# State space outputs, second normalisation, dispatch, expert tiles and last sum in one stage

## The chip, the cores and the metric

The kernel runs on one core of a Trainium2 chip. The metric is the device time of one execution in microseconds (us). PE is TensorE, DVE VectorE, ACT ScalarE, POOL GpSimd, SP SyncE, the engine that issues most of the plain DMAs.

## The reference

Sixteen sequences of 256 tokens with 128 features pass through four layers. Each adds to x the normalised output of its sublayer: `x = x + layernorm(f(layernorm(x)))`. The sublayers are a differential attention, two blocks of window attention with feed forward, a state space model, and a mixture of experts. The change lies in the last two:

```python
# state space: u = x W_in' + b_in; h_t = h_(t-1) A + u_t Bm'
return jnp.einsum('bsn,hn->bsh', hs, C) + D

# mixture of experts, 8 experts, 2 for each token
logits = xt @ router_w.T
topk_vals, topk_idx = jax.lax.top_k(logits, 2)
g = sigmoid(topk_vals);  g = g / (g.sum(-1, keepdims=True) + 1e-10)
for e in range(8):
    ge = jnp.sum(jnp.where(topk_idx == e, g, 0), axis=-1)
    h = silu(xt @ w_gate[e]) * (xt @ w_up[e])
    out = out + ge[:, None] * (h @ w_down[e])
```

## The kernel before

X and F are two arrays in SBUF that hold all tokens: 32 tiles of 128 tokens. A group is four tiles, so there are eight groups. Everything is float32. The program is a row of blocks. In a block each engine has its own list of instructions, worked off in order, with semaphores between engines; a block ends when all its engines are done, and only then does the next one begin. POOL waits at the end of its lists for the DMAs it has issued.

The four blocks at the end are these.

**State space** (`state_space`, L1351). PE turns and projects F, then eight levels of a doubling scan run over the states `Hs`. The last loop makes the outputs: for each of 16 sequences PE makes two products of the states with C into a PSUM buffer (L1467), and DVE adds D and writes F (L1422). The buffers are two, so PE and DVE alternate.

**Second normalisation and dispatch** (`dispatch`, L1511). Per group g: `inner.statistics` of F on DVE (L627 to L634), `power` on POOL for 1/sqrt (L620), `shifts` on DVE (L639), `apply` on ACT (L647), the addition to X on DVE (L1634), the same normalisation of X (`outer`) into `pay`, then `turn` on PE (L1664), ACT's move of it to SBUF (L1655), `route` on PE (L1672), `choose` on DVE (L1580 to L1607: the two best experts, one-hot rows, running counts), `ranks` on PE (L1683 to L1687) and `place` on DVE (L1612 to L1622: the row number of each token in its expert's region). Last, `send` on POOL scatters the four tiles to DRAM, `mx_rows`, once for each choice: eight indirect DMAs for a group (L1558), 64 in all. DVE goes through its parts in a loop in which each part lags the one before by a step. POOL's loop is `inner.power(g)`, `outer.power(g - 2)`, `send(g - 5)`. PE's is `turn(g)`, `route(g - 1)`, `ranks(g - 2)`. POOL ends by waiting for all sends.

**Expert tiles** (`mixture_of_experts`, L1714). DVE first makes a table of which expert and which rows belong to each of 72 slots of 128 rows (`tiles_of_experts`, L1786 to L1811, which raises `listed`), then the gates (L1816 to L1826). SP waits for `listed`, loads row numbers to registers, and loads tiles (`mx_xin`, L1764). Per slot: PE turns the tile (L1919), one product gives gate and up (L1926), ACT makes silu (L1881), DVE multiplies (L1848), PE turns (L1934), ACT moves, PE makes the down product (L1942), DVE copies it to `y` (L1855), and POOL scatters it to `mx_results` (L1773), four buffers of `y` being in turn. POOL ends by waiting for all scatters.

**Last sum.** SP loads both results of each token (L1980, L1981), ACT and DVE weigh and add them (L2003, L2016), the sum is normalised, POOL adds it to X (L1994), SP stores (L1984).

## Time and profile before

| | us |
|---|---|
| median of 3 runs | 2083.77 |
| lowest and highest | 2082.64, 2086.82 |
| the profiled execution | 2089.91 |
| its span, first to last instruction | 2088.1 |
| busy: PE, DVE, ACT, POOL | 1708.9, 1544.3, 1361.4, 876.0 |

The page cuts the span into 40 equal slices of 52.2 us; a digit is the busy share in tenths:

```profile
PE   4999999999999936999996977999996939242990
DVE  2888989889898856999995566999995573632444
ACT  2888888888888844888884325888884252411554
POOL 3555655556555543333231232323331240473554
PEclk9999999999999966999998988999998978555995
```

PEclk is the TensorE clock granted, in tenths of 2.4 GHz, so a 5 is 1.2 GHz. The last seven or eight slices are the blocks told of above. In an answer of the trace an instruction stands with its start, its duration, its engine and line, output and inputs, and in brackets the idle time of its engine just before it and what ended that.

### The profile page before, as it was taken

Reading aid. Unit: us, or ns where it says so; the run is one execution under the profiler, and the core shown is the slowest. Engines: PE = TensorE matmul, PEld = TensorE weight load, DVE = VectorE, ACT = ScalarE, POOL = GpSimd, SP = SyncE. Lnnn points to the kernel's source line nnn. Section 1 sums busy time; section 2 is a strip of 40 time slices with the busy share of each in tenths; the row PEclk is TensorE's granted clock in tenths of the full one; section 3 lists DMA queues with packets and bytes.
Section 4 is the critical chain, followed back from the end, with each engine's and each line's share of the span. In section 5 each row is a group of like instructions: output and inputs, shape, how many; then the busy total and the mean of one; then the engine's idle time right before and its main releaser. Section 6 shows DMA issues by size and latency. Waiting matters only on the chain. (4 is left out here: it accounts for less than half of the span.)

```text
span 2088.1 us, 39231 instructions
## 1 busy us (share of the span) xinstructions
PE 1708.9 (82%) x12344; PEld 1128.4 (54%) x12410; DVE 1544.3 (74%) x4156; ACT 1361.4 (65%) x4708; POOL 876.0 (42%) x816
## 2 busy tenths in 40 slices
PE   4999999999999936999996977999996939242990
PEld 2555555555555514777774545777774515241660
DVE  2888989889898856999995566999995573632444
ACT  2888888888888844888884325888884252411554
POOL 3555655556555543333231232323331240473554
PEclk9999999999999966999998988999998978555995
DMA  6990000000000000000000100000001100012324
GB/s 203 185 180 6 2 2 1 2 2 1 2 2 2 2 0 6 16 16 11 17 16 20 30 12 6 12 16 16 17 11 25 30 2 1 15 47 53 83 64 129
DMA packets 102525, 65.90 MB, mean 32 GB/s; under 512 B 27698, under 2 KB 93874, under 8 KB 102322
## 3 DMA queue, kind: packets, MB, share of 16 engines
q1 hardware_dynamic: 97970, 54.40, 13.1%
q0 software_dynamic: 4352, 8.99, 1.3%
q8 instruction: 103, 1.69, 0.4%
q14 instruction: 100, 0.82, 0.1%
HBM read 19.50 MB, written 30.24 MB: 24 GB/s over the span
## 5 line engine op out<-in xcount | busy, mean ns | idle before, releaser
L411 ACT ACTIVATE a_E<-a_psS,a_nm 128x128 f32<-128x128 f32 (+1 forms) x1028 | 418.8, 428 | 31.3 <-DVE a_nm L245 28.9
L216 POOL TENSOR_SCALAR a_aT<-a_dT 128x384 f32<-128x384 f32 x256 | 309.4, 1208 | 299.1 <-PE a_psO L529 187.5
L245 DVE TENSOR_REDUCE a_nm<-a_psS 128x2 f32<-128x256 f32 (+1 forms) x514 | 260.2, 547 | 43.7 <-PE a_psS L496 43.0
L492 PE MATMUL a_psS<-a_kT,a_qm 32*128 32x128 f32 (+1 forms) x2064 | 240.6, 351 | 5.6 <-issue 3.7
L270 DVE SCALAR_TENSOR_TENSOR a_d<-a_E,a_cf 128x128 f32<-128x128 f32 (+1 forms) x512 | 219.3, 468 | 27.9 <-DVE a_cf L259 1.4
L411 ACT ACTIVATION_READ_ACCUMULATOR a_E<-a_psS,a_nm 128x1 f32 x1028 | 219.9, 214 | 0.0
L830 POOL TENSOR_TENSOR b0rn<-b0ss,minus_half 128x16 f32<-128x16 f32 x36 | 107.1, 2976 | 224.1 <-DVE b0ss L866 224.1
L830 POOL TENSOR_TENSOR b1rn<-b1ss,minus_half 128x16 f32<-128x16 f32 x36 | 107.1, 2976 | 223.3 <-DVE b1ss L866 223.3
L420 ACT ACTIVATE a_dT<-a_psT 128x384 f32<-128x384 f32 x256 | 126.7, 495 | 74.4 <-PE a_psT L505 71.4
L492 PEld LDWEIGHTS a_psS<-a_kT,a_qm 32*128 32x128 f32 x2064 | 136.6, 186 | 55.8 <-issue 35.6
L505 PE MATMUL a_psT<-ident,a_d 128*128 128x128 f32 x768 | 132.4, 281 | 6.2 <-DVE a_d L270 0.3
L505 PEld LDWEIGHTS a_psT<-ident,a_d 128*128 128x128 f32 x768 | 87.7, 141 | 34.7 <-DVE a_d L270 28.4
L496 PE MATMUL a_psS<-causal,identb 128*128 128x256 bf16 x516 | 101.8, 279 | 0.0
L1773 POOL DMA_INDIRECT mx_results<-mx_y,mx_targetu x72 | 68.6, 953 | 72.3 <-DVE mx_y L1855 63.5
L964 ACT ACTIVATE b0E<-b0psS,b0nm 128x128 f32<-128x128 f32 x260 | 91.8, 376 | 10.0 <-DVE b0nm L894 10.0
L964 ACT ACTIVATE b1E<-b1psS,b1nm 128x128 f32<-128x128 f32 x260 | 91.8, 376 | 8.7 <-DVE b1nm L894 8.7
L1077 PE MATMUL b0psQ<-wqk,b0hT 128*128 128x512 f32 x148 | 81.3, 676 | 16.9 <-DVE b0part L875 12.0
L1077 PE MATMUL b1psQ<-wqk,b1hT 128*128 128x512 f32 x148 | 80.5, 670 | 16.7 <-DVE b1part L875 11.3
L1848 DVE TENSOR_TENSOR mx_h<-mx_psG,mx_sl 128x256 f32<-128x256 f32 x72 | 30.6, 425 | 72.3 <-issue 37.8
L1046 PEld LDWEIGHTS b0psS<-b0kT,b0qm 128*128 128x128 f32 x528 | 72.1, 198 | 18.2 <-issue 16.3
L1046 PEld LDWEIGHTS b1psS<-b1kT,b1qm 128*128 128x128 f32 x528 | 71.8, 197 | 18.2 <-issue 16.3
L518 PE MATMUL a_psO<-a_dT,a_vp 128*32 128x256 f32 x516 | 81.2, 393 | 0.6 <-ACT a_dT L420 0.6
(353 smaller groups left out, 4392.5 us busy)
## 6 DMA issues: line engine op xcount, KB each, us to landing
mx_rows<-mx_blank SPq DMA_DIRECT2D x9, 2080.0 KB, 32.3
mx_xin<-mx_rows SPq DMA_DIRECT2D x72, 65.0 KB
b0v<-b0v SPq DMA_DIRECT2D x34, 128.0 KB, 2.3
b1v<-b1v SPq DMA_DIRECT2D x34, 128.0 KB
F<-mx_results SPq DMA_DIRECT2D x8, 256.0 KB, 4.8
mx_second<-mx_results SPq DMA_DIRECT2D x8, 256.0 KB, 5.3
out_dram<-X SPq DMA_DIRECT2D x8, 256.0 KB, 2.3
f0z<-F SPq DMA_DIRECT2D x9, 128.0 KB
```

The costliest lines, as they stand in the source:

```text
L216: pool.tensor_scalar(aT[:, s, :], dT[:, s, :], 0.0, None, ALU.max).then_inc(positived.sem, 1)
L245: ins = dve.tensor_reduce(nm[:, s, t, :], psS[:, s, :, (0, P)[t]:(P, 384)[t]], axis=AX.X, op=ALU.max, negate=True)
L270: ins = dve.scalar_tensor_tensor(out=d[:, s, c0:c1], in0=E[:, s, 1, c0:c1], scalar=cf[:, s, t:t + 1], in1=E[:, s, 0, c0:c1], op0=ALU.mult, ...
L411: ins = act.activation(E[:, s, m, c0:c1], psS[:, s, m, c0:c1], ACT.Exp, bias=nm[:, s, t, m:m + 1], accum_out=Z[:, p, h, t, m:m + 1])
L420: act.activation(dT[:, s, :], psT[:, s, 0:384], ACT.Copy).then_inc(evaced.sem, 1)
L492: pe.matmul(psS[:, s, m, c0:c1], qm[rows, p, a, r, t * P:(t + 1) * P], kT[rows, p, a, 0:c1 - c0], start=(t == 0), stop=False)
L496: ins = pe.matmul(diagonal, identb[:, :], causal[:, :].unsqueeze(1).broadcast_to([P, 2, P]), start=False, stop=True)
L505: ins = pe.transpose(psT[:, s, c * P:(c + 1) * P], d[:, s, c * P:(c + 1) * P], ident[:, :])
L830: pool.tensor_tensor(rn[:, t, :], ss[:, t, :], minus_half[:, 0:2 * H], ALU.pow).then_inc(rn_ready.sem, 1)
L964: ins = act.activation(E[:, s, n, :], psS[:, s, n * P:(n + 1) * P], ACT.Exp, bias=nm[:, s, n:n + 1], accum_out=Z[:, s, n:n + 1])
L1046: ins = pe.matmul(psS[:, s, n * P:(n + 1) * P], qm[:, p, g, n].rearrange("p j q -> p (j q)"), kT[:, p, g, KEYS[n]:KEYS[n] + P], start=Fals ...
L1077: ins = pe.matmul(psQ[:, n * W:(n + 1) * W], hT[:, p, t * P:(t + 1) * P], wqk[:, n * W:(n + 1) * W], start=True, stop=True)
```

## The change

Everything from the state space's outputs on becomes one block. `dispatch` is gone; `state_space` ends with the scan and leaves its states in `states`. `mixture_of_experts` does the rest: 

- The outputs are made two sequences at a time, which is one group: `outputs(b)` on PE and `outputs(g)` on DVE, which goes on to the group's statistics.
- The order of the first three groups (LEAD) is written out on DVE, ACT, PE and POOL. Behind that DVE's loop is: outer shifts of g + 2, inner shifts of g + 3, choose(g + 1), outputs(g + 4), place(g + 1), residual(g + 3). PE's is: outputs, route(g + 1), turn(g + 2), ranks(g + 1). POOL's is: send(g), inner power of g + 4, outer power of g + 3.
- Behind the loops the table of slots, the gates and the slots follow on each engine in its own list. SP waits for `listed`, loads registers, then waits for all sends (`sent`) ahead of its first load; it waits for all scatters ahead of loading results. POOL waits for neither.
- Means and variances (`mv`) have a buffer for each group. PSUM is shared: the router's buffers are those of the expert tiles, and those of the outputs serve as `psT` and `psC`.

```diff
-        self.mv = ctx.enter_context(nc.sbuf_tensor(name + "mv", [P, 2, G, 2], FP32))
+        self.mv = ctx.enter_context(nc.sbuf_tensor(name + "mv", [P, self.groups, G, 2], FP32))
...
-            for b in range(BATCH):
-                dve.wait_ge(y_full, b + 1)
-                dve.tensor_tensor(f_of(b), psX[:, b % 2, 0:T].rearrange("p (t n) -> p t n", t=QT),
-                                  dv[:, :].unsqueeze(1).broadcast_to([P, QT, D]), ALU.add).then_inc(y_ready, 1)
...
+        psX = psG = ps("psG", [P, 2, 512])
+        psR = psH = ps("psH", [P, 2, 512])
+        psK = psY = ps("psY", [P, 2, 512])
+        psO = ps("psO", [P, 2, 512])
+        psT, psC = psO[:, 0, :], psO[:, 1, :]
...
+        @block.sync
+        def _(sp):
+            sp.wait_ge(listed, 1)
+            for i in range(SLOTS):
+                if i % SHARE == 0:
+...
+                if i == 0:
+                    sp.wait_ge(sent, 16 * 2 * TILES)
...
+            for k in range(4):
+                sp.wait_ge(scattered[k], 16 * (SLOTS // 4))
+            o = out.rearrange("b (t p) d -> p (b t) d", p=P)
+            for g in range(GROUPS):
+                sp.dma_start(ln.tiles(F, g), result(0, g)).then_inc(fetched[g], 16)
...
         @block.gpsimd
-            for g in range(GROUPS + 5):
+            for g in range(LEAD):
+                inner.power(pool, g)
+            outer.power(pool, 0)
+            outer.power(pool, 1)
+            inner.power(pool, LEAD)
+            outer.power(pool, 2)
+            pool.wait_ge(filled, 16 * fills)
+            for g in range(GROUPS):
+                send(g)
+                if g + 4 < GROUPS:
+                    inner.power(pool, g + 4)
+                if g + 3 < GROUPS:
+                    outer.power(pool, g + 3)
...
-            pool.wait_ge(sent, 16 * 2 * TILES)
...
         @block.vector
+            def outputs(g):
+                for b in (2 * g, 2 * g + 1):
+                    dve.wait_ge(o_full, b + 1)
+                    dve.tensor_tensor(F[:, QT + b * QT:QT + (b + 1) * QT, :],
+                                      psO[:, b % 2, 0:T].rearrange("p (t n) -> p t n", t=QT),
+                                      dv[:, :].unsqueeze(1).broadcast_to([P, QT, D]), ALU.add).then_inc(o_used, 1)
+                dve.wait_ge(o_used, 2 * g + 2)
+                inner.statistics(dve, g)
...
+            outputs(0)
+            outputs(1)
+            inner.shifts(dve, 0)
+            outputs(2)
+            inner.shifts(dve, 1)
+            residual(0)
+            inner.shifts(dve, 2)
+            residual(1)
+            outer.shifts(dve, 0)
+            outputs(3)
+            outer.shifts(dve, 1)
+            residual(2)
+            choose(0)
+            place(0)
+            for g in range(GROUPS):
+                if g + 2 < GROUPS:
+                    outer.shifts(dve, g + 2)
+                if g + 3 < GROUPS:
+                    inner.shifts(dve, g + 3)
+                if g + 1 < GROUPS:
+                    choose(g + 1)
+                if g + 4 < GROUPS:
+                    outputs(g + 4)
+                if g + 1 < GROUPS:
+                    place(g + 1)
+                if g + 3 < GROUPS:
+                    residual(g + 3)
+            tiles_of_experts()
+            gates()
...
         @block.scalar
+            for g in range(LEAD):
+                inner_apply(g)
+            outer_apply(0)
+            move_turned(0)
+            outer_apply(1)
+            for g in range(GROUPS):
+                if g + 1 < GROUPS:
+                    move_turned(g + 1)
+                if g + 2 < GROUPS:
+                    outer_apply(g + 2)
+                if g + 3 < GROUPS:
+                    inner_apply(g + 3)
...
         @block.tensor
+            for b in range(2 * LEAD + 2):
+                outputs(b)
+            turn(0)
+            route(0)
+            turn(1)
+            ranks(0)
             for g in range(GROUPS):
+                if g + 4 < GROUPS:
+                    outputs(2 * g + 8)
+                    outputs(2 * g + 9)
+                if g + 1 < GROUPS:
+                    route(g + 1)
+                if g + 2 < GROUPS:
+                    turn(g + 2)
+                if g + 1 < GROUPS:
+                    ranks(g + 1)
+            pe.wait_ge(seen_ready, GROUPS + 1)
+            pe.matmul(psC[:, 0:NE], c["ones"][:, :], seen[:, GROUPS, :], start=True, stop=True).then_inc(counted, 1)
+            pe.wait_ge(listed, 1)
...
```

## Rows read from the trace of the kernel before

**Rows 1.** Windows by stage: stretch, length, busy PE PEld DVE ACT POOL, clock, DMA, GB/s.

```profile
1775.40:1809.05 33.65, 8.53 (x38) 7.90 (x38) 23.24 (x157) 13.92 (x34) 11.33 (x10) 0.50 0.00 1
1809.05:1902.40 93.35, 30.16 (x138) 29.36 (x138) 30.95 (x215) 16.17 (x38) 68.60 (x70) 0.50 0.14 45
1902.40:1909.46 7.06, 0.00 (x0) 0.00 (x0) 0.00 (x0) 0.00 (x0) 0.00 (x0) 0.50 0.03 9
1909.46:1916.38 6.92, 0.57 (x2) 0.50 (x2) 5.86 (x16) 1.54 (x2) 0.00 (x0) 0.50 0.00 1
1916.38:2043.34 126.96, 121.24 (x648) 81.09 (x648) 50.43 (x174) 62.67 (x181) 68.60 (x72) 0.97 0.28 76
2043.34:2051.05 7.71, 0.00 (x0) 0.00 (x0) 0.00 (x0) 0.00 (x0) 0.00 (x0) 0.57 0.02 9
2051.05:2088.10 37.05, 0.00 (x0) 0.00 (x0) 23.30 (x112) 22.73 (x64) 18.91 (x16) 0.50 0.64 171
```

**Rows 2.** Timeline of DVE, first outputs and statistics: start, duration, instruction, idle before.

```profile
1762.28 0.87 DVE L1422 TENSOR_TENSOR F<-s_psX,s_wD 128x256 f32<-128x256 f32 x2 [0.80 <-PE s_psX L1467]
...
1775.39 0.20 DVE L1625 COPY mx_pay<-mx_token 128x32 f32<-128x32 f32 x1 [0.64 <-PEq L1362]
...
1775.48 0.87 DVE L627 BATCH_NORM_STATS2 n2ist<-F 128x6 f32<-128x128 f32 x4
...
1776.88 0.86 DVE L627 BATCH_NORM_STATS2 n2ist<-F 128x6 f32<-128x128 f32 x4
```

**Rows 3.** Timeline, one group's way from residual over router to placing.

```profile
1780.14 0.69 DVE L1634 TENSOR_TENSOR X<-X,F 128x512 f32<-128x512 f32 x1 [0.25 <-ACT F L647]
...
1794.06 0.19 DVE L1580 COPY d_lo<-d_psR 128x32 f32<-128x32 f32 x1 [4.40 <-PE d_psR L1672]
...
1796.53 0.86 DVE L627 BATCH_NORM_STATS2 n2ist<-F 128x6 f32<-128x128 f32 x4
...
1804.40 0.55 PEld L1683 LDWEIGHTS d_psK<-d_both,mx_tri 128*128 128x128 f32 x2
...
1806.18 0.61 PE L1687 MATMUL d_psK<-mx_seen,mx_ones 128*128 128x32 f32 x2
...
1807.13 0.18 DVE L1612 TENSOR_TENSOR d_rank<-d_psK,mx_region 128x32 f32<-128x32 f32 x1
...
1860.85 0.60 ACT L1655 ACTIVATE d_xT<-d_psX 128x512 f32<-128x512 f32 x1 [0.72 <-PE d_psX L1664]
```

**Rows 4.** Timeline, POOL's sends: first, ninth, 49th, last.

```profile
1809.05 1.24 POOL L1558 DMA_INDIRECT mx_rows<-mx_pay,d_posu  x1 [7.76 <-issue]
...
1821.38 1.57 POOL L1558 DMA_INDIRECT mx_rows<-mx_pay,d_posu  x1 [0.18 <-issue]
...
1882.49 0.96 POOL L1558 DMA_INDIRECT mx_rows<-mx_pay,d_posu  x1 [3.78 <-DVE d_posu L1622]
...
1901.44 0.95 POOL L1558 DMA_INDIRECT mx_rows<-mx_pay,d_posu  x1 [0.30 <-issue]
```

**Rows 5.** Groups by line and form, 1775 to 1909 us: all 64 sends.

```profile
L1558 POOL DMA_INDIRECT mx_rows<-mx_pay,d_posu x64 | 62.4, 975 | 32.4 <-issue 26.0 <-DVE d_posu L1622 6.4
```

**Rows 6.** Waits of DVE, 1809 to 1903 us: total, times, longest.

```profile
DVE d_rank L1612 <- remote: 8.2, 2, 5.5
```

**Rows 7.** Timeline, SP's first load of token tiles.

```profile
1916.38 8.65 SPq L1764 DMA_DIRECT2D mx_xin<-mx_rows  x15
```

**Rows 8.** Window behind the last send, columns as in rows 1.

```profile
1903.50:1904.00 0.50, 0.00 (x0) 0.00 (x0) 0.00 (x0) 0.00 (x0) 0.00 (x0) 0.50 0.00 0
```

**Rows 9.** Timeline, one scatter (POOL) and the copy four slots later (DVE).

```profile
2027.00 0.95 POOL L1773 DMA_INDIRECT mx_results<-mx_y,mx_targetu  x1 [0.79 <-DVE mx_y L1855]
...
2032.98 0.28 DVE L1855 COPY mx_y<-mx_psY 128x128 f32<-128x128 f32 x1
```

**Rows 10.** Timeline, a gate and up product on PE, early and late in the expert tiles.

```profile
1922.50 1.91 PE L1926 MATMUL mx_psG<-m_experts,mx_xT 128*128 x2
...
2024.62 1.02 PE L1926 MATMUL mx_psG<-m_experts,mx_xT 128*128 x2
```

More of the change, by code:

```diff
@@ L1359, in state_space @@
     ident = consts["ident"]
[L1360 removed]
+    win, bin_, bm, am, amT = (w[k] for k in ("W_in", "b_in", "Bm", "A", "AT"))
     with ExitStack() as ctx:
@@ L1575, in _, with residual @@
             own_steps = Steps(dve, own)
+            def outputs(g):
[6 more added lines that the diff above has]
+                inner.statistics(dve, g)
+            def residual(g):
+                dve.wait_ge(applied, g + 1)
+                xs = inner.tiles(X, g)
+                dve.tensor_tensor(xs, xs, inner.tiles(F, g), ALU.add).then_inc(added, 1)
+                dve.wait_ge(added, g + 1)
+                outer.statistics(dve, g)
             def choose(g):
@@ new lines, in aim @@
+            def aim(n):
+                mark, last = own_steps.mark, own_steps.last
+                share = slice(n * SHARE, (n + 1) * SHARE)
+                ring = slice(n * SHARE % RING, n * SHARE % RING + SHARE)
+                for i in range(n * SHARE, (n + 1) * SHARE):
+                    x_of(dve, i)
+                mark(dve.tensor_tensor(other[:, share], xin[:, ring, D + 1], expert[:, share], ALU.not_equal))
+                last()
+                mark(dve.scalar_tensor_tensor(out=target[:, share], in0=other[:, share], scalar=float(TILES * P),
+                                              in1=xin[:, ring, D], op0=ALU.mult, op1=ALU.add))
+                last()
+                dve.tensor_tensor(targetu[:, share], target[:, share], c["trash"][:, share], ALU.min)\
+                   .then_inc(aimed, 1)
@@ new lines, in _ @@
+            tiles_of_experts()
+            gates()
+            gate_up(0)
+            for i in range(SLOTS + 1):
+                if i % SHARE == 0 and i < SLOTS:
+                    aim(i // SHARE)
+                if i + 1 < SLOTS:
+                    gate_up(i + 1)
+                if i >= 1:
+                    move_y(i - 1)
+            for g in range(GROUPS + 1):
+                if g < GROUPS:
+                    dve.wait_ge(weighted, g + 1)
+                    for t in range(NT):
+                        z = ln.tiles(F, g)[:, t, :]
+                        ins = dve.scalar_tensor_tensor(out=z, in0=second[:, g * NT + t, :],
+                                                       scalar=sg[:, g * NT + t, 1:2], in1=z, op0=ALU.mult, op1=ALU.add)
+                    ins.then_inc(summed, 1)
+                    dve.wait_ge(summed, g + 1)
+                    ln.statistics(dve, g)
+                if g >= 1:
+                    ln.shifts(dve, g - 1)
@@ L1644, in _, with inner_apply @@
         @block.scalar
         def _(act):
[L1646 to L1655 removed]
+            def inner_apply(g):
+                inner.apply(act, g, inner.tiles(F, g)).then_inc(applied, 1)
@@ new lines, in _ @@
+            outer_apply(0)
+            move_turned(0)
+            outer_apply(1)
+            for g in range(GROUPS):
+                if g + 1 < GROUPS:
[4 more added lines that the diff above has]
+                    inner_apply(g + 3)
+            act.wait_ge(hot_ready, GROUPS)
+            act.activation(sg[:, :, :], top[:, :, 0:2], ACT.Exp, scale=-1.0).then_inc(expd, 1)
+            move_x(0)
@@ new lines, in _ @@
+            silu(0)
+            for i in range(SLOTS):
+                if i % 2 == 0 and i + 2 < SLOTS:
+                    move_x(i // 2 + 1)
+                if i + 1 < SLOTS:
+                    silu(i + 1)
+                move_h(i)
+            act.wait_ge(gated, 1)
+            for g in range(GROUPS + 2):
+                if g < GROUPS:
+                    act.wait_ge(fetched[g], 32)
+                    for t in range(NT):
+                        ins = act.activation(ln.tiles(F, g)[:, t, :], ln.tiles(F, g)[:, t, :], ACT.Copy,
+                                             scale=sg[:, g * NT + t, 0:1])
+                    ins.then_inc(weighted, 1)
+                if g >= 2:
+                    ln.apply(act, g - 2, second[:, of(g - 2), :]).then_inc(normal, 1)
@@ L1657, in _, with outputs @@
         @block.tensor
         def _(pe):
+            def outputs(b):
+                n, j = divmod(b, SEQ)
+                group = slice(NS * n, NS * n + NS)
+                if b >= 2:
+                    pe.wait_ge(o_used, b - 1)
+                for t in range(QT):
+                    ins = pe.matmul(psO[:, b % 2, t * P:(t + 1) * P], states[group, j, t * P:(t + 1) * P], cT[group, :],
+                                    start=True, stop=True)
+                ins.then_inc(o_full, 1)
             def turn(g):
```

583 lines of the change are left out of this document (219 added, 364 removed).

## The prediction

> **What bounds the kernel now.** I read the page first: its slices show that PE is near 90% until about 1690 us, and that behind this every engine has holes. The change touches only that last part, so the windows by stage come next [rows 1]. They show four things. The second normalisation with the dispatch lasts from 1775.40 to 1902.40 us, and its larger part, 93.35 us, is the time from POOL's first send to its last. Behind it lie 7.06 us in which nothing computes, then 6.92 us in which only the table of expert tiles is made, then 126.96 us of expert tiles with PE busy for 121.24. Then come 7.71 us of nothing, and 37.05 us of the last sum. Ahead of all this stand the 16 output products of the state space, which the timeline shows as a stage of their own, 1762.28 to the next block's first instruction at 1775.39 [rows 2].
>
> The second look is at what POOL, which sets the end of the dispatch, waits for. One send occupies 1.263 us: from the 49th to the 64th there are 15 intervals in 18.95 us [rows 4], with DVE idle. Eight make a group, 10.1 us. From the first to the ninth send there are 12.33 us, so the two rs powers in between cost 2.2 us, 1.1 each [rows 4]. POOL idled for DVE's places only 6.4 us in all [rows 5]. So 64 sends plus powers are the floor there, and what can be gained is an earlier first send and whatever stands between the last send and the first load.
>
> **The first send.** Before, it starts at 1809.05 [rows 4]. For the changed kernel I lay DVE's written order out with measured pieces. The recurrence's last addition ended 0.80 before the first output addition, at 1761.48, and a block change costs 0.64 [rows 2]; DVE's first output addition then starts 0.80 later, at 1762.9. One call of outputs(g) is two additions (0.87 together), a gap of 0.04, and one statistic, 1.40 from start to start [rows 2]: 2.3 us. One residual(g) is an addition of 0.69 plus the same 1.40 with its gap: 2.1 us [rows 2, 3]. A shift is below 0.1. Three outputs, two residuals and three shifts put outer.shifts(0) at 1774.3. From an outer shift to the router's result DVE waited 4.40 us (ACT's apply, PE's turn and route) [rows 3]; in the new order ACT's move to SBUF stands in this chain too, with its wait of 0.72 and its 0.60 [rows 3], so choose(0) starts at 1774.3 + 4.4 + 1.3 = 1780.0. By then DVE has done outputs(3) and residual(2) (to 1778.9), so they are free. Choosing takes 2.47 us (1794.06 to 1796.53), the hot rows being ready 2.1 in; the ranks take 2.4 on PE (1804.40 to 1806.79) [rows 3]; from the first instruction of place to the first send it is 1.9 us (1807.13 to 1809.05) [rows 3, 4]. That gives 1780.0 + 2.1 + 2.4 + 0.1 + 1.9 = 1786.5. **Part one: 22.5 us earlier.** Some 13 of these are the outputs stage, which no longer stands alone: PE's eight first products run ahead under DVE's statistics, and the other eight under the sends.
>
> **The sends.** Three more powers fall between first and last send (nine in place of six), as the first send is earlier: +3.3. The 6.4 us of idle go if DVE stays ahead. While powers are coupled (they stand behind send(g) in POOL's queue, and DVE's next shifts wait for them), DVE's turn is shifts 0.16, choose 2.47, outputs 2.3, place 0.8, residual 2.1, and a wait of about 0.6 for the ranks, which stand behind turn(g+2) on PE (the turn ends 3.1 into the DVE's turn, the ranks 2.4 later, and place could start at 4.9): 8.5 us, against the 10.1 of POOL's eight sends. The cover is thus 1.6 us a group, and where it is gone, each us of DVE costs one. PE has the two products and the route ahead of turn and ranks, and both waits are long fulfilled. The last three groups have no powers behind the sends: place(7) comes near 1859, eight us before its send is due. The span becomes 93.35 - 6.4 + 3.3 = 90.3, ending at 1876.8. **Part two: 3.1 us.**
>
> **From the last send to the first load.** Before, these are 13.98 us (1902.40 to 1916.38) [rows 1, 7]. The table (6.92 us) now runs on DVE behind place(7), near 1860 to 1868, under the last sends; if that cover is gone it costs up to 6.9. Exp's table load and the gates lie there too, and SP's register loads stand ahead of its wait for the sends. What is left is the landing of the last send. The trace shows no wait for a send alone, so I bound it. From below: bytes stop 1.1 us behind the issue's end [rows 8], and some half us for the semaphore makes 1.6. From above: the scatter issued until 2027.95 must have landed before the copy at 2032.98, which did not wait for it: 5.0 [rows 9]. I take the middle, 3.3, since the empty 7.06 are nearer to the upper end and hold a block change as well; with 0.3 for SP, 3.6. **Part three: 13.98 - 3.6 = 10.4 us** (8.7 to 12.1).
>
> The Trainium skill, DMA: Bandwidth & Descriptors, section on the anatomy of one DMA on the gpsimd path, gives about 2.0 us of fixed cost to a DMA, mostly the write receipt. Counted from the issue's start that would be some 1.2 us behind its end, an estimate from that page, and the whole would come out about 4 us lower than my sum; the empty 7.06 us do not contradict it, but do not show it.
>
> **The expert tiles.** Same instructions, same PSUM banks in another naming, POOL's scatters unchanged: 126.96 us [rows 1]. PE has a pause ahead of them as before, so its cold start should be the same. **Zero.**
>
> **Results to last sum.** POOL's wait and the block change go; SP waits itself for the same last scatter. Before 7.71 us [rows 1], now 3.6 by the same landing: **4.1 us** (2.4 to 5.8). The last sum keeps its 37.05; eight slots in place of two for mean and variance change no duration.
>
> **How the numbers follow.** 22.5 + 3.1 + 10.4 + 4.1 = 40.1 us. Against the profiled execution: 2088.1 - 40.1 = 2048.0 of span. The profiled execution took 2089.91 with what lies around the span, 6.1 above the median of the three runs, 2083.77. The differences are of stages that don't depend on that, so the forecast is 2083.77 - 40.1 = 2043.7 us. Chance 0.68.
>
> **Rivals.**
> First, DVE late for POOL. In the late dispatch DVE waited 8.2 us in two waits for something the profile calls remote, once 5.5 [rows 6], though PE had finished; this is where most of POOL's 6.4 came from. With a cover of 1.6 a group such pauses could fall into the coupled part. All of the idle back gives 2043.7 + 6.4 = 2050; the full 8.2 twice over, less cover, about 2056. For it: the sends now begin 22 us sooner, under more DVE work. Against: in the last three groups the cover is 8 us. Chance 0.18.
> Second, POOL slowed by DVE beside it: each send longer than 1.263. If an output addition (0.43) held a send for its whole length, the eight under the sends cost 3.5, with the statistics of four groups (1.4 each) 9: 2053. Against: the first eight sends, beside DVE's statistics, kept the pace of the late ones beside an idle DVE (12.33 less two powers is the same 10.1) [rows 4]. Chance 0.07. The Trainium skill names such a mechanism, in SBUF — State Buffer, section on the two separate sides: GpSimd and a DVE instruction in a two-port mode lock each other out of a shared port, and descriptors written on GpSimd starve. By that rule the change would be hurt; the trace speaks against it here.
> Third, the barrier's removal doing nothing: the table comes late behind a stalled DVE and the landing is at its upper end. 6.9 + 3.4 back: 2054. Chance 0.03.
> Fourth, slower: PE stays at its low clock in the expert tiles. Early in the stage a gate and up product took 1.91, late 1.02 [rows 10]. The stage is PE's, 121.24 us in 72 slots or 1.7 each [rows 1], so a slot at the low clock of 1.2 GHz adds some 1.5. From 27 slots on the gain is gone; all 72 would give about 2150. Before, the stage's mean grant was 0.97 [rows 1], so the rise came early, and nothing in PE's work there changes. Chance 0.03.
> No measurable change (0.2% is 4.2 us, about what a measurement of this kernel can tell): 0.01.
>
> Chances: faster 0.96, same 0.01, slower 0.03. The range takes the landing's bounds on both sides (3.4 each way), two us for the layout of the first groups, two for the median, and the first two rivals above: 2036.5 to 2056.
>
> **What would show it.** The first send near 25 us behind the recurrence's last addition, where it was 47.6; 64 sends within 90 us without a wait for a place; the first load 2 to 5 us behind the last send; the first fetch of results the same behind the last scatter; the tile stage at 127 us. A coupled turn above 12.4 us would refute the cover; a first load later than 5.3 us behind the last send, the landing; a tile stage over 130 us, the zero there.

## The result, and the profile after

The changed kernel takes 2049.78 us, the median of 4 runs (2048.32 to 2053.39); the kernel before takes 2083.97 us beside it (4 runs, 2082.64 to 2086.82). The ratio is 0.9837, 95% interval 0.9819 to 0.9854: 1.6% faster, 34 us. Forecast were 2043.7 us, in a range of 2036.5 to 2056. Run again on another chip (below), it gave 0.9841 (0.9826 to 0.9856).

The profiled execution took 2051.13 us, its span is 2049.3. It is shown by the same stretches as [rows 1]: from the recurrence's last addition to the first send, the sends, to SP's first load of tiles, to the end of the last scatter, to SP's first fetch, to the end of POOL's last addition, to the end. The columns are stretch, length, busy time of PE, PEld, DVE, ACT and POOL, PE's granted clock, DMA share, GB/s.

```profile
1761.87:1786.36 24.49, 14.64 (x67) 12.61 (x67) 18.39 (x108) 10.21 (x25) 8.39 (x8) 0.56 0.00 1
1786.36:1878.92 92.56, 39.74 (x177) 37.81 (x176) 48.70 (x296) 21.34 (x50) 71.71 (x73) 0.50 0.14 46
1878.92:1880.60 1.68, 0.00 (x0) 0.00 (x0) 0.00 (x0) 0.00 (x0) 0.00 (x1) 0.50 0.12 40
1880.60:2007.96 127.36, 121.00 (x648) 80.60 (x648) 49.81 (x171) 62.77 (x181) 69.07 (x72) 0.97 0.28 76
2007.96:2009.31 1.35, 0.00 (x0) 0.00 (x0) 0.00 (x0) 0.00 (x0) 0.00 (x0) 0.50 0.14 49
2009.31:2043.13 33.82, 0.00 (x0) 0.00 (x0) 23.29 (x112) 22.74 (x64) 18.93 (x16) 0.50 0.66 176
2043.13:2049.34 6.21, 0.00 (x0) 0.00 (x0) 0.00 (x0) 0.00 (x0) 0.00 (x1) 0.50 0.20 58
```

Beside before and the forecast, in us:

| stretch | before | forecast | after | after less before |
|---|---|---|---|---|
| recurrence's last addition to first send | 47.57 | 25.0 | 24.49 | -23.1 |
| first send to end of last | 93.35 | 90.3 | 92.56 | -0.8 |
| to the first load | 13.98 | 3.6 | 1.68 | -12.3 |
| expert tiles | 126.96 | 126.96 | 127.36 | +0.4 |
| last scatter to first fetch | 7.71 | 3.6 | 1.35 | -6.4 |
| last sum, to the end | 37.05 | 37.05 | 40.03 | +3.0 |

With 0.4 us by which the recurrence ended later, these make the 38.8 us between the two spans. The medians lie only 34.2 apart: the profiled execution of before was 6 us above its median, that of after 1.4. Three lines want an explanation: the sends hardly gained, the last sum lost 3 us that no step of mine held, and the two gaps closed further than any landing time I had assumed.

The way to the first send, on the timeline (start, duration, engine, instruction, idle time before it in brackets):

```profile
1763.20 0.87 DVE L1662 TENSOR_TENSOR F<-mx_psO,s_wD 128x256 f32<-128x256 f32 x2 [0.48 <-PE mx_psO L1927]
...
1774.32 0.15 DVE L639 SCALAR_TENSOR_TENSOR n2oshift<-n2omv,n2ors 128x4 f32<-128x4 f32 x1
...
1779.92 0.19 DVE L1678 COPY mx_lo<-mx_psH 128x32 f32<-128x32 f32 x1 [1.07 <-PE mx_psH L1944]
```

The first outer shift stands at 1774.32 (forecast 1774.3), choose(0) at 1779.92 (forecast 1780.0), the first send at 1786.36 (forecast 1786.5). As the recurrence ended 0.39 us later than in the trace of before (1761.87 for 1761.48), each station came 0.4 to 0.5 us sooner behind it than forecast. In all these 24.49 us DVE waits four times, the longest times 2.0 us for the first ranks and 1.1 us for the router.

Among the sends, one wait was in no forecast. The last ranks and the last group's first send:

```profile
1859.18 0.61 PE L1959 MATMUL mx_psY<-mx_seen,mx_ones 128*128 128x32 f32 x2
...
1867.27 0.19 DVE L1710 TENSOR_TENSOR mx_rank<-mx_psY,mx_region 128x32 f32<-128x32 f32 x1 [9.43 <-remote]
1869.02 0.96 POOL L1621 DMA_INDIRECT mx_rows<-mx_pay,mx_posu  x1 [2.45 <-DVE mx_posu L1720]
```

PE's matmul is listed as over at 1859.79, but DVE starts at 1867.27, and POOL idles 2.45 us for it. In [rows 6] DVE's d_rank waited in the same manner, 5.5 us once, and the 6.4 us of POOL's idle time in [rows 5] came from that.

The block ends, last. By line and engine's sequencer, with min/median/max ns, the drain with which POOL leaves a block: the dispatch (L1519), the tiles (L1714) and the last sum (L1709) of before, then the only one of after.

```profile
L1519 POOLq DRAIN  x1: 5298/5298/5298, 1903.9 to 1903.9; - x1
```
```profile
L1714 POOLq DRAIN  x1: 5927/5927/5927, 2044.9 to 2044.9; - x1
```
```profile
L1709 POOLq DRAIN  x1: 1374/1374/1374, 2084.1 to 2084.1; - x1
```
```profile
L1507 POOLq DRAIN  x1: 7278/7278/7278, 2041.8 to 2041.8; - x1
L1507 SPq COMPARE_BRANCH  x1: 38/38/38, 2045.5 to 2045.5; - x1
```

A drain's record begins while POOL's last instruction still runs. In before's last block POOL's addition ran through 1.29 of the 1.37 us, so the drain itself is 0.1, and the end of that kernel came 2.70 us behind POOL's last addition:

```profile
2085.40:2088.10 2.70, 0.00 (x0) 0.00 (x0) 0.00 (x0) 0.00 (x0) 0.01 (x1) 0.50 0.47 134
```

In after the addition ended at 2043.13 and the drain at 2049.12, 5.98 us later, at the very end: SP's last wait, for the output's landing, was over at 2045.5, and the kernel ended at 2049.3. The two blocks of before that hold sends or scatters had 5.30 and 5.93 us. So the suspicion before the experiments: **not the barrier and not the landing, but POOL's drain is what a block end costs here, and the change removed two and moved one to the end.**

### The profile page after: what moved, and what is told of

Read it like the earlier page. It is cut to its first block and busy times, and to the rows that moved or that the text cites. A ratio compares the mean times of both kernels' runs of the same rounds, so it can differ in the third digit from the quotient of the medians.

```text
span 2049.3 us, 39274 instructions
## 1 busy us (share of the span) xinstructions
PE 1719.8 (84%) x12410; PEld 1128.4 (55%) x12410; DVE 1544.9 (75%) x4156; ACT 1363.4 (67%) x4708; POOL 877.9 (43%) x816
## 5 line engine op out<-in xcount | busy, mean ns | idle before, releaser
L1046 PEld LDWEIGHTS b0psS<-b0kT,b0qm 128*128 128x128 f32 x528 | 71.9, 198 | 18.2 <-issue 16.3
L1046 PEld LDWEIGHTS b1psS<-b1kT,b1qm 128*128 128x128 f32 x528 | 71.9, 197 | 18.2 <-issue 16.3
```

What stands on the lines that cost most here:

```text
L1046: ins = pe.matmul(psS[:, s, n * P:(n + 1) * P], qm[:, p, g, n].rearrange("p j q -> p (j q)"), kT[:, p, g, KEYS[n]:KEYS[n] + P], start=Fals ...
```

## Experiments

Each is compared with the kernel before by runs on the same chip; chips differ by some us, so ratios are compared, and stretches of the traces.

**1. The last sum in a block of its own.** The changed kernel, one block end put back:

```
-            for k in range(4):
-                sp.wait_ge(scattered[k], 16 * (SLOTS // 4))
...
+            for k in range(4):
+                pool.wait_ge(scattered[k], 16 * (SLOTS // 4))
...
+        first_blocks.close()
+        block = ctx.enter_context(nc.Block())
```

> The changed kernel, with only the last sum put back into a block of its own (POOL waits for the scatters before the block ends, as before the change). Theory A: a block in which POOL issued software DMAs ends with a POOL drain of 5.3 us (seen in the trace of before: POOL's wait for the sends was over at 1903.75, its drain stood until 1909.22), whatever is still in flight. Then the gap from the last scatter's end to the first fetch goes from 1.36 us to about 7.7, and the tail from POOL's last addition to the end goes from 6.17 us to about 2.7, because the last block holds no software DMA: net +2.9 us, about 2052.7. Rival B, the gap before was mostly the landing of the scatter, and the long tail of the changed kernel has another cause (the out transfer): the gap grows by a block change of 0.7 us, the tail stays at 6.2: +0.7 us, about 2050.5. Rival C, the barrier costs 6.35 us and the tail is the out transfer's: gap 7.7, tail 6.2, about 2056.

Measured: 2052.42 us, ratio 0.9854 (0.9835 to 0.9873). The gap, the last sum and the tail, and the two drains:

```profile
2004.77:2012.51 7.74, 0.00 (x0) 0.00 (x0) 0.00 (x0) 0.00 (x0) 0.00 (x0) 0.60 0.02 8
2012.51:2046.95 34.44, 0.00 (x0) 0.00 (x0) 23.39 (x112) 22.73 (x64) 18.87 (x16) 0.50 0.63 173
2046.95:2049.67 2.72, 0.00 (x0) 0.00 (x0) 0.00 (x0) 0.00 (x0) 0.00 (x1) 0.50 0.47 131
```
```profile
L2007 POOLq DRAIN  x1: 5952/5952/5952, 2006.3 to 2006.3; - x1
...
L1507 POOLq DRAIN  x1: 1362/1362/1362, 2045.7 to 2045.7; - x1
```

Both sides of theory A: the gap is 7.74 and the tail 2.72. The drain has moved from the end to the block end, it hasn't vanished. B and C fall, since each kept the tail at 6.2. The loss in time against the changed kernel, 0.0017 in the ratio, lies within the two intervals; the trace's stretches carry the verdict.

**2. Both block ends put back**, so that only the merged outputs and the order are left of the change (POOL waits for the sends at the end of the dispatch's block, as before).

> The changed kernel with both block ends put back, so that only the merge of the state space outputs with the dispatch and the written-out order stay. Theory A: first send about 24.5 us behind the recurrence's last addition and the sends 92.6 us long, as in the changed kernel; from the last send's end to the first load 13.5 to 14.5 us in place of 1.68 (landing 1.35, drain 5.3, table of tiles 6.5, block change), then the gap of the last scatter 7.7 and the tail 2.7: about 12.3 + 2.9 = 15.2 us above the changed kernel, 2065. Rival: the barriers were hidden behind the landing of the transfers (gap 4 to 5 us more at each): 2057 or less. Rival: part of the early first send is lost when the blocks are apart: above 2070.

Measured: 2060.44 us, ratio 0.9893 (0.9876 to 0.9909).

```profile
1763.54:1788.02 24.48, 14.63 (x66) 12.60 (x67) 18.39 (x108) 10.20 (x25) 8.39 (x8) 0.56 0.01 1
1788.02:1878.27 90.25, 39.38 (x175) 37.41 (x174) 41.76 (x278) 19.80 (x48) 71.52 (x73) 0.50 0.14 47
1878.27:1892.26 13.99, 0.57 (x2) 0.50 (x2) 5.87 (x16) 1.54 (x2) 0.00 (x0) 0.50 0.02 5
...
2018.74:2026.45 7.71, 0.00 (x0) 0.00 (x0) 0.00 (x0) 0.00 (x0) 0.00 (x0) 0.53 0.02 9
```

Every stretch came as theory A has it: 24.5, 14.0, 7.7, a tail of 2.7. Against the changed kernel the two gaps and the tail make 15.2 us; from the recurrence to the end the trace is 13.6 us longer than that of experiment 5, as its tiles and its last sum were somewhat shorter. The medians make 13 (2060.44 to 2047.39, with before at 2080.47 and 2081.28 beside them), the two ratios (0.9893 and 0.9841) 11. The 2065 of the expectation counted from the first chip's times, on which everything is some 3 us longer. The two merges of blocks are thus worth some 11 to 14 us and the first part of the change some 20 to 22. The sends took 90.25 us here, the 90.3 of the prediction.

**3. Who waits for the landing.** The kernel before, with POOL's two waits moved to SP in the next block:

```
-            pool.wait_ge(sent, 16 * 2 * TILES)
...
+                    if i == 0:
+                        sp.wait_ge(sent, 16 * 2 * TILES)
...
-                for k in range(4):
-                    pool.wait_ge(scattered[k], 16 * (SLOTS // 4))
...
+            for k in range(4):
+                sp.wait_ge(scattered[k], 16 * (SLOTS // 4))
```

> The kernel before the change, with one thing altered: POOL doesn't wait at the two block ends for its sends and scatters to land; SP waits for them at the head of the next block instead. Theory A (the drain is the price, 5.3 us, and it isn't the wait for the landing): the gaps stay within 1.5 us of 13.98 (last send's end to first load) and 7.71 (last scatter's end to first fetch), and the time within 0.1% of before, about 2083. Rival: POOL's drain is long only because it comes behind a wait, or the landing is what costs: 13.98 goes to about 8.7 and 7.71 to about 2.5, together 10 us, about 2073.

Measured: 2081.65 us (10 runs) beside 2080.47 (13 runs), ratio 0.9997 (0.9987 to 1.0007): no difference.

```profile
1811.36:1898.48 87.12, 30.17 (x138) 29.36 (x138) 30.24 (x215) 16.17 (x38) 68.28 (x70) 0.50 0.15 48
1898.48:1910.95 12.47, 0.57 (x2) 0.50 (x2) 5.86 (x16) 1.54 (x2) 0.00 (x1) 0.50 0.02 6
...
2038.38:2045.04 6.66, 0.00 (x0) 0.00 (x0) 0.00 (x0) 0.00 (x0) 0.00 (x1) 0.62 0.03 10
```
```profile
L1519 POOLq DRAIN  x1: 20427/20427/20427, 1883.4 to 1883.4; - x1
```

The gaps shrank by 1.5 and 1.05 us, the landing alone, which now runs beside the drain; the drain stayed: its record, which now begins ahead of the last sends, ended at 1903.8, 5.3 us behind the last send. So of the 13.98 us of [rows 1, 7] the landing was 1.4, the drain 5.3, the table 6.9, block change and issue the rest. The two small gains are no larger than the interval. The first row says something else: the sends of the kernel before took **87.12 us** here, not 93.35. That is less by 6.2, nearly all of the 6.4 of [rows 5], which thus were no property of the kernel.

**4. The late signals.** PE kept busy behind the last route and behind the counts:

```
+            def spin(n):
+                pe.wait_ge(xTd_ready, GROUPS)
+                for _ in range(n):
+                    pe.matmul(psX[:, 0, 0:P], ident[:, :], ident[:, :], start=True, stop=True)
...
+                if g == GROUPS - 2:
+                    spin(8)
...
+            spin(32)
```

> The changed kernel with 8 spare matmuls on PE behind the last route (ahead of the last ranks) and 32 behind the matmul of the counts, results unused. In the changed kernel DVE got the last ranks at 1867.24 although PE's matmul is listed as ended at 1859.79, and place(7) came so late that POOL idled 1.6 us before its last eight sends. Theory P: PE's result reaches the others late when no further matmul follows it. Then with the spare matmuls place(7) starts at about 1861, POOL's idle time for it goes, and the time falls by 1.6 us (to 2048). Theory S: the signals are late because POOL issues sends without a break (no power between them): place(7) still starts at about 1867 and the time stays at 2049.8. Below both: the spare matmuls delay the last ranks by 1.7 us at most, hidden.

Measured: 2047.15 us, ratio 0.9835 (0.9815 to 0.9854). The last ranks reached DVE at 1855.04, as PE's matmul ended, and the sends took 90.78. But the kernels of experiments 1 and 2, without spare matmuls, showed the same in their traces, so this one tells P and S apart no better than chance: inconclusive. The better question is whether the wait belongs to the program at all.

**5. The changed kernel once more.**

> The changed kernel itself once more, as the measure for the three others. It also tells what the late signals are: in its first trace DVE got PE's last ranks at 1867.24, 7.1 us behind the listed end of the matmul, and the sends took 92.6 us; in the trace of before two such waits of 4 us made the sends 93.3 us. The trace of before with SP waiting (87.1 us), and the three variants of the changed kernel (90.3 to 90.8) had none. Theory E, the late signals belong to single executions: sends of 90.3 us this time, the idle time ahead of send(7) only the 0.3 of every send. Theory K, they belong to this program: again 92 to 93 us. The other stretches as in the first trace: 24.5 to the first send, gap 1.4 to 1.7, tail 6.2.

Measured: 2047.39 us, ratio 0.9841 (0.9826 to 0.9856).

```profile
1757.16:1781.65 24.49, 14.63 (x67) 12.60 (x67) 18.40 (x109) 10.19 (x25) 8.38 (x8) 0.56 0.01 1
1781.65:1872.04 90.39, 39.76 (x177) 37.84 (x176) 48.59 (x296) 21.34 (x50) 71.64 (x73) 0.50 0.14 47
...
2002.40:2037.23 34.83, 0.00 (x0) 0.00 (x0) 23.39 (x112) 22.73 (x64) 18.87 (x16) 0.50 0.62 171
2037.23:2043.43 6.20, 0.00 (x0) 0.00 (x0) 0.00 (x0) 0.00 (x0) 0.00 (x0) 0.50 0.20 57
```
```profile
1852.22 0.61 PE L1959 MATMUL mx_psY<-mx_seen,mx_ones 128*128 128x32 f32 x2
...
1852.87 0.19 DVE L1710 TENSOR_TENSOR mx_rank<-mx_psY,mx_region 128x32 f32<-128x32 f32 x1 [1.96 <-PE mx_psY L1959]
```

Theory E: the same program, and the ranks are taken the moment they are there. 90.39 us is the length of the sends when nothing is late, and the late signals belong to single executions. Where they occur, it is in the last four groups' stretch, and POOL loses 2 to 6 us there. Five of the fourteen traces have them: before, after, and the variants of experiments 8 (93.26 us in place of some 88.6), 9 and 11. What delays them is open.

**6. The outputs back in the state space's stage**, the written-out order and the single block kept.

> The changed kernel with the state space outputs put back into the state space stage (16 products and additions in a stage of their own, a block end behind them), everything else as changed, the written-out order too, in which DVE then has the statistics alone where outputs stood. My theory of part one: the separate stage costs its 13.1 us and moves the block change; DVE saves four pairs of additions of 0.9 us ahead of the first send. First send 34.5 us behind the recurrence's last addition (24.5 + 13.7 - 3.6), at most 38; sends 90.3 us as before; gap and tail as changed; so 10 to 13 us above the changed kernel. Rival: DVE wasn't the bound ahead of the first send (PE, ACT and POOL's turns were), so the additions were covered: 38 us.

Measured: 2059.06 us, ratio 0.9895 (0.988 to 0.9911), 11.7 us above the changed kernel on the same chip.

```profile
1757.77:1792.79 35.02, 20.58 (x98) 19.01 (x98) 22.23 (x118) 10.09 (x25) 7.94 (x8) 0.54 0.00 1
```

35.02 where 34.5 were expected; the sends were 90.39 as in experiment 5. The rival (38, the additions covered) falls: DVE's additions do count ahead of the first send.

**7. The uniform loops of before, with outputs merged and the single block kept.** The core of the edit, on DVE (POOL and ACT have their loops of before, PE has outputs, turn, route and ranks in one loop):

```
+            for g in range(GROUPS + 6):
+                if g < GROUPS:
+                    outputs(g)
+                if 1 <= g <= GROUPS:
+                    inner.shifts(dve, g - 1)
+                if 2 <= g < GROUPS + 2:
+                    residual(g - 2)
...
+                if 5 <= g < GROUPS + 5:
+                    place(g - 5)
```

> The changed kernel with outputs merged and no block ends, but with the uniform loop of before on POOL, DVE, ACT and PE (a send only behind the power of five groups on) in place of the written-out order. My theory: before had 47.57 us to the first send, of which 13.1 were the outputs stage; the merged outputs add up to six pairs of additions of 0.9 us on DVE: first send 35 to 39 us behind the recurrence's last addition; with six powers between the sends in place of nine the sends take 87.1 us; gap and tail as changed. Together 8 to 12 us above the changed kernel. Rival: DVE was idle enough for all additions: 34.5 us, 7 above. Rival: DVE's turn with outputs passes POOL's eight sends of 10.1 us: sends above 88 us.

Measured: 2063.68 us, ratio 0.9922 (0.9906 to 0.9938), 16.3 us above the changed kernel on the same chip. The expectation was wrong. First the windows, then DVE's waits up to the first send (line waited for: us in total, times, longest):

```profile
1758.53:1802.59 44.06, 20.96 (x94) 18.71 (x94) 27.68 (x164) 14.13 (x34) 11.78 (x11) 0.53 0.00 1
1802.59:1891.20 88.61, 32.56 (x148) 31.57 (x148) 38.66 (x241) 17.71 (x40) 68.72 (x70) 0.50 0.15 48
```
```profile
DVE mx_lo L1674 <- PE mx_psH L1921: 8.8, 2, 4.4
DVE F L1658 <- PE mx_psO L1904: 5.0, 3, 4.0
```

The first send comes 44.06 us behind the recurrence, not 35 to 39. DVE waits 4.0 us for products that stand behind a turn in PE's own queue, and the turn waits for ACT. I had counted DVE's additions only. The sends took 88.6 us, not 87.1: ahead of the second and the third group POOL waits a little for DVE, whose turn with outputs is longer than eight sends, as the second rival had it.

**8. The same with the products one group ahead on PE.**

```
+            outputs(0)
+            outputs(1)
             for g in range(GROUPS + 5):
-                if g < GROUPS:
-                    outputs(2 * g)
-                    outputs(2 * g + 1)
+                if g + 1 < GROUPS:
+                    outputs(2 * g + 2)
+                    outputs(2 * g + 3)
```

> The variant with the uniform loops (old_order), with one thing altered: on PE the two output products of group g+1 stand ahead of turn and route of the iteration, in place of those of group g. In old_order the first send came 44.06 us behind the recurrence, not the 35 to 39 I expected, and DVE waited 4.03 and 0.43 us for products that stood behind a turn in PE's queue, and twice 4.4 us for the router. Theory Q (PE's own queue did it): with the products ahead the first send comes at 39 to 40 us, 4 to 5 us earlier, and the time falls as much, to about 2059. Rival: DVE only moves its waiting to the router's result, which depends on its own turn: the first send stays within 1.5 us of 44.

Measured: 2065.04 us, ratio 0.9889 (0.9872 to 0.9906), against 0.9922 for experiment 7 (on this chip the kernel before takes 2087.53 us).

```profile
1760.24:1799.64 39.40, 21.74 (x97) 19.35 (x98) 27.88 (x167) 14.14 (x34) 11.78 (x10) 0.54 0.00 1
```

39.40, in the middle of theory Q's range: PE's queue was the 4.7 us that I had missed. The ratio fell by 0.0033, some 7 us where 5 were expected, which the two intervals allow. In this trace itself nothing was won up to the end, as it has the longest of the late signals:

```profile
1862.67 0.61 PE L1936 MATMUL mx_psY<-mx_seen,mx_ones 128*128 128x32 f32 x2
...
1881.24 0.19 DVE L1706 TENSOR_TENSOR mx_rank<-mx_psY,mx_region 128x32 f32<-128x32 f32 x1 [14.50 <-remote]
```

PE's last ranks were over at 1863.28, and DVE took them 18.0 us later.

**9. One software DMA in the last block.** (The expectations call POOL's indirect DMAs, the sends and scatters, software DMAs.) Experiment 1's kernel with, at the head of POOL's last block,

```
+            pool.indirect_dma_start(
+                rows, bass.IndirectOffsetOnAxis(ap=posu[:, GROUPS - 1, 1, NT - 1:NT], axis=0),
+                pay[:, TILES - 1, :], None).then_inc(sent, 16)
+            pool.wait_ge(sent, 16 * (2 * TILES + 1))
```

> The variant with the last sum in a block of its own, with one send repeated by POOL as the first instruction of that last block (the same row data to the same places of the dispatch buffer, which nobody reads any more), and POOL's wait for its landing right behind it, 30 us before the block ends. Without it the last block ended 2.7 us behind POOL's last addition. Theory A1 (one software DMA anywhere in a block is enough for the long drain): POOL's last drain stands 6 us beyond its last addition and the tail is 6.2 us again: 3.5 us slower than without. Theory A2 (the drain's length grows with the number of software DMAs in the block, 64 gave 5.3 and 72 gave 5.9): the tail stays at 2.7 to 2.8. Theory A3 (it counts only from the last software DMA on): the tail stays at 2.7, as that was 30 us ago; the changed kernel, whose last scatter lies 36 us before its end, speaks against it.

Measured: 2051.46 us, ratio 0.9831 (0.9814 to 0.9847). The tail stayed at 2.71 us. A1 falls: one is not enough. POOL's last drain record is 1459 ns, where it was 1362, so 0.1 us more. A2 and A3 forecast the same here; against A3 stands, as it says, the changed kernel, with 5.98 us of drain 35 us behind its last scatter.

**10 and 11. Half of the sends, and all of them twice**, both from experiment 2's kernel.

```
-                    for choice in range(2):
+                    for choice in range(1):
```

> The variant with three blocks, with the sends of the second choice left out (32 sends in the dispatch's block in place of 64) and the second result fetched from the first's place: half of the dispatch and the second expert's share of the output are left out, so its total time says nothing. Looked at is POOL's drain at the end of the dispatch's block, 5.30 us behind 64 sends (5.93 behind 72 scatters, 0.1 us and nothing more in a last block that held one send, 5.98 in the changed kernel, whose one block holds 136). Theory N (a cost for each software DMA in the block, 0.083 us each by the first two): 2.65 us. Theory F (a fixed cost as soon as there are more than a few): 5.3. The drain behind the scatters stays 5.93 in both.

```
             pool.wait_ge(sent, 16 * 2 * TILES)
+            for g in range(GROUPS):
+                send(g)
+            pool.wait_ge(sent, 16 * 4 * TILES)
```

> The variant with three blocks, with all 64 sends issued a second time, the same data to the same places, once the first 64 have landed: 128 software DMAs in the dispatch's block. Some 82 us longer for the sends themselves, which is not looked at. Theory N without a limit: the drain at the end of that block lasts 10.6 us. Theory N with a limit near 72 (which would make the 5.98 of the changed kernel's 136 fit): 5.9 to 6.0 us. Theory F: 5.3 as before.

One execution of each. The drain at the end of the dispatch's block, with 32 sends, and with 128:

```profile
L1801 POOLq DRAIN  x1: 2685/2685/2685, 1850.2 to 1850.2; - x1
```
```profile
L1804 POOLq DRAIN  x1: 1297/1297/1297, 1968.2 to 1968.2; - x1
```

2.68 us for 32 sends, 5.30 for 64, 5.93 for 72 scatters: 0.083 us each, theory N. But 128 gave 1.30, which none of the three had. Something of it must be paid earlier in that block: POOL pauses once, for 3.16 us in place of the usual 0.30, ahead of the 114th send,

```profile
1947.99 0.96 POOL L1595 DMA_INDIRECT mx_rows<-mx_pay,mx_posu  x1 [3.16 <-issue]
```

and 1.30 us would be 16 sends at 0.083. In the changed kernel too the 114th software DMA of the block has a pause of 1.77 us ahead of it, in the tiles, where POOL isn't what the end waits for:

```profile
1972.07 0.97 POOL L1643 DMA_INDIRECT mx_results<-mx_y,mx_targetu  x1 [1.77 <-issue]
```

The same 1.77 stands there in every kernel whose sends and scatters share a block (experiments 1, 4 to 9 and 12), and in none with a block end between them (before, experiments 2 and 3). The drain behind these 136 is 5.98 all the same (5.95 in experiment 1), that of 72 and not of 24. So the price for each holds from 1 to 72, and what counts beyond that is open.

**12. A faster version.** The last two groups' additions of the last sum on DVE, so that POOL is done before the end and its drain runs under the last transfers:

```
-                if g >= 1:
+                if 1 <= g < GROUPS - 1:
                     pool.wait_ge(normal, g)
...
+            dve.wait_ge(done, GROUPS - 2)
+            for g in (GROUPS - 2, GROUPS - 1):
+                dve.wait_ge(normal, g + 1)
+                dve.tensor_tensor(ln.tiles(X, g), ln.tiles(X, g), second[:, of(g), :], ALU.add).then_inc(done, 1)
```

> The changed kernel with the additions of the last two groups of the last sum on DVE in place of POOL, so that POOL's last instruction is the power of group 7, some 3.5 us before the end of its last addition. Theory A (POOL's drain of about 6 us runs from POOL's own last instruction, and it is what ended the kernel): POOL's drain ends at about 6.0 us behind the power, DVE's last addition ends 0.6 us earlier than POOL's did, the out transfer lands 2.3 us behind that, and the span falls by 3.0 to 3.6 us: about 0.16% under the changed kernel. Rival B (the drain starts for all engines together when the last of them is done): the tail stays 6.2 us behind the last addition, and only 0.6 us is won. Rival C (the tail is the out transfer's): 0.6 us as well, but the tail row shows the transfer landing last.

Measured: 2042.69 us (5 runs, 2042.34 to 2044.71), ratio 0.9815 (0.9802 to 0.9829), against 2047.39 of the changed kernel on the same chip.

```profile
2004.03:2037.21 33.18, 0.00 (x0) 0.00 (x0) 24.67 (x114) 22.73 (x64) 16.37 (x14) 0.50 0.69 179
2037.21:2040.51 3.30, 0.00 (x0) 0.00 (x0) 0.00 (x0) 0.00 (x0) 0.00 (x0) 0.50 0.40 114
```
```profile
L1507 POOLq DRAIN  x1: 7033/7033/7033, 2033.2 to 2033.2; - x1
...
L1507 SPq COMPARE_BRANCH  x1: 38/38/38, 2039.5 to 2039.5; - x1
```

Theory A: POOL's last power ended at 2034.30, the drain 5.98 us later, at 2040.28, and B's tail of 6.2 us behind the last addition is 3.30. From the first fetch to the end it is 36.48 us, against 40.03 and 41.03 in the two traces of the changed kernel. The output has landed at 2039.5, so the drain still is what ends last, by 0.7 us. The intervals of the two ratios overlap a little, their medians are 0.23% apart, and the traces agree; it is the fastest version measured.

## Why the prediction was right, and where not

**The first send: right.** 22.5 us forecast, 23.1 measured, and each station of the laid-out order within 0.6 us, counted from the recurrence's last addition. What the prediction said of its make-up ("some 13 of these are the outputs stage, which no longer stands alone") was too simple, as the two halves alone show, by the time from recurrence to first send:

| | outputs in their own stage | outputs merged |
|---|---|---|
| uniform loops | 47.57 | 44.06 (39.40 with products ahead on PE) |
| written-out order | 35.02 | 24.49 |

The order alone brings 12.6 us, merging alone 3.5 to 8.2, both together 23.1. Merging pays in full only where few outputs stand ahead of the first send: in the uniform loops they are those of six groups on DVE and PE, in the written-out order those of four.

**The sends: right in their length, wrong in the gain.** The 90.3 us came out as 90.25 and 90.39. The step that failed is "the 6.4 us of idle go if DVE stays ahead": it took an idle time of one execution for a property of the kernel. Without it the kernel before has 87.12 us, and the nine powers between sends in place of six make the stretch 3.3 us longer. So the step's sign is wrong: +3.3, not -3.1. A hint was there: a wait for "remote" beside a PE that had long finished [rows 6] was the only thing of this size that no part of the program explained. The profiled execution of before also lay 6.1 us above the median of its runs, but that alone would prove little: the execution traced in experiment 2 lay 4.7 us above its median with no late signal in it. There the part ahead of the change was the longer one; the recurrence's last addition ended at 1763.54, and at 1758.95 in experiment 4 on the same chip. That the unchanged kernel's ordinary runs are free of the idle time rests on experiment 3's trace, and on the sum below, which meets the medians only without it; a second trace of the unchanged kernel is missing.

**The two gaps: right in kind, mis-sized.** Forecast 3.6 us each behind last send and last scatter, measured 1.5 to 1.7 and 1.35; in before too POOL's wait for the sends was over 1.4 us behind the last one's end (1902.40 to 1903.8), so the trace did show the landing that "no wait for a send alone" denied. I took the middle of 1.6 to 5.0. The lower bound was nearly right, 0.2 us too high: the bytes had stopped by 1.1 us [rows 8], and for the half us of the semaphore, which stood in no row, 1.4 leaves 0.3. The upper one [rows 9] was loose. What drew me to the middle was that the empty 7.06 us of [rows 1] looked like landing. They were 1.4 of landing and 5.3 of drain. The Trainium skill, DMA: Bandwidth & Descriptors, section on the anatomy of one DMA on the gpsimd path, puts a DMA's fixed cost at about 2.0 us. A send here was landed about 2.3 us after its start (0.95 and 1.4), so the estimate from that page was the better one, and weighing it lower than the empty stretch was a mistake.

**The last sum: wrong.** "The last sum keeps its 37.05" forgot that a block's end is part of the sum: its last drain was 0.1 us only because that block held no software DMA. Merged, the end carries 5.98 us of drain, and the tail grew from 2.7 to 6.2: +3.5 us for a term that was put at nothing. The prediction had looked for what a removed barrier hides and not for what the barrier had already settled.

**The table and the rivals.** The table of tiles ran under the last sends, as forecast (nothing of it is left in the gap of 1.5 to 1.7 us). DVE late for POOL (0.18) did not happen by DVE's own turn; in single executions POOL did wait for it, by the late signals. POOL slowed by DVE (0.07) did not happen: 64 sends were busy for 62.5 us, mean 977 ns, beside a DVE with half as much work again (48.7 us of 92.6), after 62.4 and 975 [rows 5]:

```profile
L1621 POOL DMA_INDIRECT mx_rows<-mx_pay,mx_posu x64 | 62.5, 977 | 27.2 <-issue 18.3 <-DVE mx_posu L1720 8.9
```

The rule of the Trainium skill, SBUF — State Buffer, section on the two separate sides, by which GpSimd and a DVE instruction in a two-port mode lock each other out, thus shows no effect with DVE's instructions of this stage. Whether any of them ran in such a mode no run here shows, so "by that rule the change would be hurt" was more than the rule says. Barriers that do nothing (0.03) fell to experiment 2, and PE's granted clock in the tiles was 0.96 to 0.97, so the slower case (0.03) did not come.

**The sum.** Forecast -40.1 us, the medians gave -34.2. Set right: -23.1 for the first send, +3.3 for the sends, -12.3 and -6.4 for the gaps, +3.0 to +4.0 for the last sum (two traces), +0.4 for the tiles: -34 to -35. The 6 us too many are the idle time (6.2) and the tail (3.5), less the 4.2 by which the gaps closed further than forecast; the rest is within the spread of the runs.

## What to carry to other kernels

Before idle time in a trace is counted as a gain, look for it in a second trace of the same program, above all where the profile names no cause for it in the program; if the first execution is slower than the median by that much, the gain may not be there, though only the second trace's stretch tells where the time went. A block in which GpSimd issued many indirect DMAs ends with a drain that grew with their number up to the 72 measured here, whoever waits for their landing: merge such a block with its neighbours, and then end GpSimd's work early, so that the drain isn't the kernel's last act. Merging a stage into the next one pays in full only with an order in which no engine's queue does more of the early stage than the first result of the late one needs.

## What was not expected of the hardware

POOL's drain at a block's end lasted 0.1 us with no indirect DMA in the block, 0.2 with one, 2.68 with 32, 5.30 with 64 and 5.93 with 72, and time since their landing does not take it away (in the changed kernel the last one had been issued 35 us earlier, and the drain was 5.98). With 128 it was 1.30, with a pause of 3.16 us ahead of the 114th; with 136 it was 5.98, with a pause of 1.77.

A result of PE reached DVE up to 18.0 us after the matmul's listed end (experiment 8; 7.5 in the first trace of the changed kernel, and at once in the second); it was seen in five of fourteen traces, only in the stretch of the last four groups' sends, when PE had little or nothing else queued, and no experiment here produced or removed it at will.
